# Token rows split into fp16 halves before storing, and turned by DMA transposes instead of TensorE, in the two mixture layers of a gated cross-attention kernel

## What is computed

```python
x = x + tanh(g_xattn[0]) * L0_xattn(layernorm(x), ctx)    # linear attention
x = x + tanh(g_ffn[0])   * L0_ffn(layernorm(x))           # 8 experts, top 2
x = x + tanh(g_xattn[1]) * L1_xattn(layernorm(x), ctx)    # softmax attention, int8 rounding
x = x + tanh(g_ffn[1])   * L1_ffn(layernorm(x))           # 16 experts, top 4
# a mixture layer, x: [2048, 256]
logits = x @ router_w.T
weights, ids = top_k(softmax(logits))
routed = sum_e w[:, e] * ((silu(x @ gate[e]) * (x @ up[e])) @ down[e])     # inner width 176
shared = sigmoid(x @ shared_gate) * ((silu(x @ sgate) * (x @ sup)) @ sdown) # inner width 704
out = routed + shared
```

## Time and profile before

| | |
|---|---|
| median of three runs | 952.78 us |
| the profiled execution: its own time | 959.28 us |
| its span, first to last instruction | 957.5 us |
| PE matmul busy | 746.1 us (78%), 5700 instructions |
| DVE busy | 686.8 us (72%) |
| ACT busy | 443.4 us (46%) |
| POOL busy | 505.3 us (53%) |
| granted TensorE clock, mean | 0.843 of full |
| DMA, mean | 127 GB/s, 121.17 MB in all |

### The profile page before, as it was taken

The page is one execution under the profiler, slowest core; times in us unless marked ns, Lnnn a source line. Parts: engine busy times, 40 slices in busy tenths (PEclk is TensorE's granted clock), DMA queues, the critical chain, the costliest instruction groups (busy, mean ns, idle before and its releaser), DMA issues.

```text
span 957.5 us, 18420 instructions
## 1 busy us (share of the span) xinstructions
PE 746.1 (78%) x5700; PEld 496.1 (52%) x5701; DVE 686.8 (72%) x1825; ACT 443.4 (46%) x1037; POOL 505.3 (53%) x607
## 2 busy tenths in 40 slices
PE   3469749678988797677777777659879999977994
PEld 1258635456664454344444444335657777754563
DVE  4868947756775777988887888738857777734467
ACT  3355335123332233888887878725123444422331
POOL 6284974566636557553554347010054545478883
PEclk9679876789999899697767676657979999978998
DMA  8034444624542213898889988821034444446444
GB/s 287 1 92 157 157 157 147 187 80 142 164 127 89 66 34 81 146 191 160 151 163 168 182 159 162 148 75 40 0 93 137 136 136 140 142 123 143 79 79 141
DMA packets 205754, 121.17 MB, mean 127 GB/s; under 512 B 146476, under 2 KB 197808, under 8 KB 205680
## 3 DMA queue, kind: packets, MB, share of 16 engines
q1 hardware_dynamic: 192816, 91.10, 39.2%
q0 software_dynamic: 12864, 29.14, 12.5%
HBM read 64.16 MB, written 32.98 MB: 101 GB/s over the span
## 4 chain that ended last, share of the span: by engine, by line
PE 35%; DVE 11%; ACT 7%; issue 6%; DVEq 4%; DMA 3%; another core or an unknown queue 2%; POOL 1%; POOLq 0%; ACTq 0%
PE PS L269 18%; PE PS L852 4%; DVE sb_wk L1450 4%; PE PS L791 3%; ACT sb_xnf L1417 3%; DMA sb_xnf<-sb_xnf 3%; PE PS L1344 2%; ACT sb_wkh L1417 2%; PE PS L815 2%; PE PS L844 2%; PE PS L407 1%; DVEq L250 1%; DVE sb_x_sb L942 1%; DVE sb_x_sb L948 1%
## 5 line engine op out<-in xcount | busy, mean ns | idle before, releaser
L673 POOL DMA_INDIRECT sb_xnf<-token_table,sb_ids x120 | 115.8, 965 | 148.7 <-DVE sb_wk L1018 62.8
L1450 DVE TENSOR_SCALAR_CACHE_REDUCE sb_wk<-PS 128x512 f16<-128x512 f32 x256 | 161.9, 684 | 3.8 <-PE PS L1344 3.8
L269 PE MATMUL PS<-sb_xnT,sb_sgu 128*128 128x512 f16 x528 | 129.5, 398 | 1.1 <-DVE sb_lg L455 0.6
L269 PE MATMUL PS<-sb_region,sb_wkh 128*128 x720 | 122.6, 321 | 4.8 <-issue 3.1
L1417 ACT ACTIVATE sb_xnf<-PS,sb_slotv 128x512 int16<-128x512 f32 x128 | 86.8, 689 | 25.5 <-DVE sb_wk L1450 21.4
L875 ACT ACTIVATE sb_wk<-PS 128x512 f32<-128x512 f32 (+1 forms) x48 | 28.6, 596 | 144.6 <-PE PS L269 123.7
L269 PEld LDWEIGHTS PS<-sb_region,sb_wkh 128*128 128x128 f16 x720 | 69.7, 100 | 47.0 <-issue 13.9
L1417 ACT ACTIVATE sb_wkh<-PS,sb_slotv 128x512 int16<-128x512 f32 x128 | 86.6, 690 | 12.4 <-DVE sb_wk L1450 9.6
L852 PE MATMUL PS<-sb_region,sb_wkh 128*128 x600 | 78.3, 277 | 8.9 <-DVE sb_wa L1031 7.3
L269 PEld LDWEIGHTS PS<-sb_xnT,sb_sgu 128*128 128x128 f16 x528 | 53.0, 102 | 60.7 <-issue 10.9
L791 PE MATMUL PS<-sb_sdn,sb_wkh 128*128 128x256 f16 x544 | 70.8, 282 | 17.4 <-DVE sb_wkh L989 15.2
(11 more groups left out here) (296 smaller groups left out, 1717.3 us busy)
## 6 DMA issues: line engine op xcount, KB each, us to landing
slot_table<-sb_wa SPq DMA_DIRECT2D x60, 256.0 KB
slot_table<-token_table SPq DMA_DIRECT2D x16, 640.0 KB
sb_stg<-gu SPq DMA_DIRECT2D x24, 352.0 KB
sb_stg<-dn SPq DMA_DIRECT2D x24, 256.0 KB
token_table<-sb_xnf SPq DMA_DIRECT2D x16, 256.0 KB, 4.7
sb_stg<-sgu SPq DMA_DIRECT2D x8, 352.0 KB
sb_x_sb<-x SPq DMA_DIRECT2D x1, 2048.0 KB, 12.3
out<-sb_x_sb SPq DMA_DIRECT2D x16, 128.0 KB
```

Of the source, the lines that this page charges most:

```text
L269: last = nc.tensor.matmul(out_, lhs(i, c), rhs(j, c), start=(c == 0 and n == 0 and not begun), stop=(c == C - 1 and n == 2 and not more))
L673: nc.gpsimd.indirect_dma_start(xg[l][:, 2 * (g % XR) + n, :], None, xw[l][:, :], bass.IndirectOffsetOnAxis(ap=ids[:, 2 * g + n:2 * g + n + ...
L1450: nc.vector.tensor_scalar(h_any[(2 * s + h) % 6], PS[:, (2 * s + h) % LB, :], LEVELS, None, ALU.add, ALU.min, accum_out=h_nb[s % 3][:, h:h ...
```

## The change

The rows are split into a high and a low fp16 half as rows, before they are stored: ACT and DVE normalise into a buffer `wk1`, ACT copies the high halves into `xnf` (now seen as fp16, 256 high and 256 low columns per token), DVE subtracts. SP then turns each pair of tiles (128 x 1024 fp16) with one DMA transpose into `xnT`, in the place of PE's transposes and of the two passes out of PSUM; after all eight it stores the rows. In the experts' loop the gathered row holds both halves, so SP turns the two tiles of a group with two DMA transposes (128 x 512 fp16 each) into a ring of four buffers, and PE's transposes, ACT's line 894 and DVE's line 1002 go. The turned product and the result get two PSUM banks each.

```diff
         def route_pe(pe, l):
             n = E[l] + 1
-            for j in range(NT // 2 + 1):
-                if j < NT // 2:
-                    at_least(pe, r_xn[l], 0, j + 1)
-                    at_least(pe, r_xd[l], 0, j + 1)
-                    at_least(pe, r_xl[l], 0, j - 1)
-                    for c in range(C):
-                        for i in range(2):
-                            last = nc.tensor.transpose(PS[:, j % 2, c * TB + i * P:c * TB + (i + 1) * P],
-                                                       xnf[:, 2 * j + i, c * P:(c + 1) * P], idf[:, :])
-                    last.then_inc(r_xT[l].sem, 1)
...
+            for j in range(NT // 2):
+                at_least(pe, x_turned[j % 4][l], 0, 16 * (j // 4 + 1))
+                at_least(pe, r_lgc[l], 0, j - 3)
+                for i in range(2):
+                    t = 2 * j + i
+                    last = mm3(PS[:, j % 4, i * n:(i + 1) * n], lambda h, c: x_cols[:, t, h, c, :],
+                               lambda h, c: rw[l][:, h, c, :])
+                last.then_inc(r_lg[l].sem, 1)
         def route_act(act, l):
...
                     t = 2 * j
-                    nc.scalar.activation(xnf[:, t, :], x_sb[:, t, :], ACT.Identity, bias=nmr[:, t:t + 1],
+                    at_least(act, r_xl[l], 0, j - 3)
+                    nc.scalar.activation(wk1[:, j % 4, 0:D], x_sb[:, t, :], ACT.Identity, bias=nmr[:, t:t + 1],
                                          scale=rstd[:, t:t + 1]).then_inc(r_xn[l].sem, 1)
                 if j >= 1:
-                    at_least(act, r_xT[l], 0, j)
-                    nc.scalar.activation(xnT[:, 0, :, (j - 1) * TB:j * TB],
-                                         PS[:, (j - 1) % 2, :].rearrange("p (c n) -> p c n", c=C), ACT.Copy).then_inc(r_xh[l].sem, 1)
+                    at_least(act, r_xn[l], 0, j)
+                    at_least(act, r_xd[l], 0, j)
+                    nc.scalar.activation(x_rows[:, 2 * j - 2:2 * j, 0, :], wk1[:, (j - 1) % 4, :].rearrange("p (t n) -> p t n", t=2),
+                                         ACT.Copy).then_inc(r_xh[l].sem, 1)
         def route_dve(dve, l):
...
                     at_least(dve, r_xh[l], 0, j + 1)
-                    nc.vector.tensor_tensor(xnT[:, 1, :, j * TB:(j + 1) * TB], PS[:, j % 2, :].rearrange("p (c n) -> p c n", c=C),
-                                            xnT[:, 0, :, j * TB:(j + 1) * TB], ALU.subtract).then_inc(r_xl[l].sem, 1)
+                    nc.vector.tensor_tensor(x_rows[:, 2 * j:2 * j + 2, 1, :], wk1[:, j % 4, :].rearrange("p (t n) -> p t n", t=2),
+                                            x_rows[:, 2 * j:2 * j + 2, 0, :], ALU.subtract).then_inc(r_xl[l].sem, 1)
         def table_dma(sp, l):
             for j in range(NT // 2):
-                at_least(sp, r_xn[l], 0, j + 1)
-                at_least(sp, r_xd[l], 0, j + 1)
+                at_least(sp, r_xh[l], 0, j + 1)
+                at_least(sp, r_xl[l], 0, j + 1)
+                at_least(sp, x_turned[j % 4][l], 0, 16 * (j // 4))
+                sp.dma_start_transpose(x_turns[:, 2 * j:2 * j + 2].rearrange("p t g n -> p (t g) n"),
+                                       x_rows[:, 2 * j:2 * j + 2].rearrange("p t h n -> p (t h n)")).then_inc(x_turned[j % 4][l].sem, 16)
+            for j in range(NT // 2):
                 sp.dma_start(token_rows(xw[l], 2 * j, 2, slice(0, D)), xnf[:, 2 * j:2 * j + 2, :]).then_inc(stored[l].sem, 16)
         def rows_dma(sp, l):
+            def turn(g):
+                at_least(sp, e_ld[l][g % XR], 0, 32 * (g // XR + 1))
+                at_least(sp, e_gu[l], 0, g + 1 - XR)
+                if g == 0:
+                    at_least(sp, s_d[l], 0, HALF)
+                for n in range(2):
+                    sp.dma_start_transpose(xT[g % XR][:, 2 * C * n:2 * C * (n + 1), :],
+                                           xg[l][:, 2 * (g % XR) + n, 0:D].bitcast(F16)).then_inc(e_xT[l][g % XR].sem, 16)
+            for g in range(XR):
+                turn(g)
+            if l == 1:
+                sp.wait_ge(table_zeroed, 16 * ZERO_PARTS)
             for g in range(NG[l]):
+                if g + XR < NG[l]:
+                    turn(g + XR)
                 at_least(sp, e_y[l], 0, g + 1)
@@ ffn_pe
-                               lambda j, c: xnT[:, j, c, b * 512:(b + 1) * 512])
+                               lambda j, c: x_cols[:, 4 * b:4 * b + 4, j, c, :])
...
-                if inside(base, s, 0, NG[l] - 1):
-                    transposes(base, s + 1)
                 if inside(base, s, 0, NG[l]):
                     e = experts(base, s)
-                    at_least(pe, e_xl[l], base, s + 1)
+                    at_least(pe, e_xT[l][s % XR], base * 8, 32 * (s // XR + 1))
                     for n in range(2):
-                        last = mm3(PS[:, 2 * u + n, 0:EG], lambda i, c: wkh[:, 2 * u + i, (2 * n + c) * P:(2 * n + c + 1) * P],
+                        last = mm3(PS[:, 2 * u + n, 0:EG], lambda i, c: xT[s % XR][:, 2 * C * n + C * i + c, :],
                                    lambda h, c: GU[l][:, bass.ds(e[n], 1), h, c, :].rearrange("p o n -> p (o n)"))
@@ block.sync
             table_dma(sp, 1)
-            sp.wait_ge(table_zeroed, 16 * ZERO_PARTS)
             rows_dma(sp, 1)
```

More of the change, by code:

```diff
@@ L289, in gated_flamingo @@
         r_xn = both("r_xn", NT // 2)
-        r_xT = both("r_xT", NT // 2)
+        x_turned = [both(f"x_turned{u}", 32) for u in range(4)]
         r_xh = both("r_xh", NT // 2)
@@ L333, in gated_flamingo @@
         e_ld = list(zip(*(both(f"e_ld{u}", 32 * len(range(u, NG[0], XR))) for u in range(XR))))
+        e_xT = list(zip(*(both(f"e_xT{u}", 32 * len(range(u, NG[0], XR))) for u in range(XR))))
         e_st = list(zip(*(both(f"e_st{u}", 16 * len(range(u, NG[0], 2))) for u in range(2))))
@@ L351, in gated_flamingo @@
         yr = [xnf_flat[:, r * 2 * D:(r + 1) * 2 * D].rearrange("p (k d) -> p k d", d=D) for r in range(CR)]
-        y_sum = [w[:, n * D:(n + 1) * D] for w, tiles in ((stg_flat, 8), (wqp32, 4), (xnf_flat[:, 12 * D:16 * D], 4))
+        y_sum = [w[:, n * D:(n + 1) * D] for w, tiles in ((stg_flat, 8), (wqp32, 4), (wkv32, 4))
                  for n in range(tiles)]
@@ L809, in ffn_pe @@
             at_least(pe, r_ids[l], 0, 1)
-            def transposes(base, s):
-                at_least(pe, e_ld[l][s % XR], base * 8, 32 * (s // XR + 1))
-                for n in range(2):
-                    for c in range(C):
-                        last = nc.tensor.transpose(PS[:, 4 + s % 2, (2 * n + c) * P:(2 * n + c + 1) * P],
-                                                   xg[l][:, 2 * (s % XR) + n, c * P:(c + 1) * P], idf[:, :])
-                last.then_inc(e_xT[l].sem, 1)
             def experts(base, s):
@@ L843, in group @@
                         for c in range(C):
-                            last = nc.tensor.transpose(PS[:, 6, (2 * c + n) * P:(2 * c + n + 1) * P],
+                            last = nc.tensor.transpose(PS[:, 5 - u, (2 * c + n) * P:(2 * c + n + 1) * P],
                                                        wk1[:, 3 - u, n * EI + c * P:n * EI + (c + 1) * P], idf[:, :])
@@ L856, in group @@
                     last.then_inc(e_d[l].sem, 1)
-            transposes(0, 0)
             steps(pe, NG[l] + 2, XR, XR, 3, group)
@@ L1093, in gated_flamingo @@
         q_iT = [w.bitcast(F16).rearrange("p (g n) -> p g n", n=P) for w in
-                (*(xnf[:, 12 + 2 * u:14 + 2 * u, :].rearrange("p t d -> p (t d)") for u in range(2)), xn32[:, 10 * D:12 * D])]
+                (*(xnf[:, 12 + 2 * u:14 + 2 * u, :].rearrange("p t d -> p (t d)") for u in range(2)), xn32[:, 14 * D:16 * D])]
         h_h = [wkh[:, 2 * u:2 * u + 2].rearrange("p a b -> p (a b)") for u in range(4)] + \
```

81 lines of the change are left out of this document (36 added, 45 removed).

## The result

The changed kernel takes 993.62 us in the median (990.41 to 1000.21, 4 runs), the kernel before 952.29 beside it: ratio 1.0434 (95% interval 1.0373 to 1.0494). It is slower, as forecast, but by 41 us where 10 were forecast, outside the range of 951 to 977. The profiled execution took 992.78 us, its span is 991.0.

The account below looks back on a forecast made before the run. PE was taken to bound layer 1's loop, POOL layer 0's, SP's queue order layer 0's routing. +22.5 - 0.5 + 1 + 0.7 - 13.7 = +10.0 us, put on the median 952.78: 963 us, range 951 to 977.

Parts of the forecast that it names:

- Routing of layer 0: Layer 0's transposes wait behind fills and loads in SP's order; logits at 182.7 instead of 154.7, 28 us late.
- Row numbers +22.5: Layer 0's row numbers come at 214.2, not 191.65: +22.5 us, between +18 and +26.
- Loop of layer 0: Layer 0's experts' loop: POOL is the bound and keeps 4.3 us a group; only -0.5 us, for the last group.
- The second rival: Layer 0's routing: fills don't hold SP, transposes go out early, kernel faster, about 943 if at 160; chance 0.06.
- Routing of layer 1: Layer 1's routing: SP is free, logits at 652.7 to 654.9 against 652.15; +1 us taken, 0 to +3.
- the two prices: Cost of one 128 x 1024 transpose: 1.23 us on SP's queue, 1.54 us with the DMA engines full.
- Loop of layer 1: Layer 1's experts' loop: PE is the bound; period 3.96 to 3.58 us, -13.7 us, with 0.7 more at its start.
- The part on DMA: Layer 1's loop: DMA needs 3.40 us a group, 97% busy at 3.52; period 3.58 taken, share above 0.8.
- The loop of layer 1 gains nothing: Rival: gather, transpose and head of line on SP make a chain of four periods of 3.96; +24, 977; chance 0.12.
- A half-size transpose costs as much as a full one: Rival, both experts' loops: 1.54 us for each half-size transpose, 4.94 us a group; about +76, 1029; chance 0.04.
- The tail: Stage 846 to 878, where PE is busy 20.1 of 32 us: taken as it is, no change.

Follow-up runs that it names:

- Both experiments on the queue: Changed kernel, layer 0's transposes issued earlier in SP's queue: 982.41 us; with stores and first four weight loads also ahead of the last zero fills: 972.41 us.
- its queue is mended: Changed kernel with layer 0's eight transposes, table stores and first four weight loads issued by SP ahead of the last four zero fills: 972.41 us, ratio 1.0168.
- a version 0.7% faster: Kernel before, PE's loop unrolled by eight steps, six of eight down products reusing gate and up's loaded registers: 953.36 us, ratio 0.9933.

## Why the prediction was right and wrong

**Routing of layer 0: right.** "The first can't be issued before 165.8": 165.80. Last transpose 182, logits 182.7: the last logits are copied at 183.27. Row numbers +22.5: the first gather is +19.8, since the steps from logits to row numbers took 28.0 us (183.27 to 211.32) where 31.5 were put. Both experiments on the queue confirm the reason, not only the number. The second rival (SP early) is what the kernel becomes if its queue is mended, and even then it isn't faster (1.0168).

**Loop of layer 0: wrong by 6.9 us.** "POOL keeps its 4.3 us" took POOL's 2.2 to 2.6 us at the drain for POOL's own. They depend on something outside POOL: with the transposes, all or half of them, they grew to 3.3 to 4.0, in every third group. From first gather to last gate and up the loop lost 6.4 us where 0.5 was to be gained. "No other engine releases it" had been read as "it is constant".

**Routing of layer 1: too cheap.** Its start is 23.4 us later than before. Less that, the first transpose goes out at 640.55 (forecast 640.1) and the last logits are copied at 655.3, where 652.7 to 654.9 were the bounds: +3.3, not +1, and outside 0 to 3. The timeline of SP's queue:
```profile
663.95 11.28 SPq L638 DMA_TRANSPOSE sb_xnT<-sb_xnf  x8
```
That is 1.41 us each, between the two prices. The stages between the two loops, combining and attention, were 2.8 us shorter than before, so that the step from layer 0's last gate and up to layer 1's first gather came out nearly as forecast (+1.2 where +1 stood), by luck.

**Loop of layer 1: the step that failed.** It is "PE: 3.96 - 0.44 = 3.52 us, or 3.41 if the gap goes as well", and from it "0.38 x 36 groups = -13.7 us". Measured: 4.23 to 4.26, and from the first gather to the first combining one the lateness grows from 27.4 to 39.8: +12.4, where -13.0 stood. That is a miss of 25.4 us; with layer 0's 6.9, the 2.7 of its routing the other way, 0.2 between, and the tail's 6.3 the other way, it makes the 23.5 us between forecast and spans. The subtraction took all the time between PE's waits for matmuls. PE's sequence also has two register loads a group, and what the change took from PE was what stood over one of them. With that load left out the period is 3.64. A sign stood in the prediction's own reading: its parts, 1.96, 0.44, 1.10, 0.44 and 0.11, add up to 4.05 and not to 3.96, since 1.96 holds time that the next record shares.

Uncovering the load doesn't explain all of it. Four transposes can cover no more than their 0.44 us, and without cover the period would have stayed at 3.87. It rose to 4.23. From the start of the last matmul ahead of gate and up to that of gate and up, the changed kernel needs 0.88 us in the mean of the window, the kernel before 0.21: 0.23 more than the transposes can account for; most of the rest stands ahead of the down product (0.20 instead of 0.11). The further 0.36 us of the period goes when the load goes, but why the load costs more in the changed kernel isn't shown. With half of the transposes the 0.88 is 0.76, so their traffic may have a part; the register arithmetic of the new wait behind the load wasn't tested by itself.

The part on DMA was sound: a period of 3.58 and a share above 0.8 were forecast for it, and 3.64 and 0.94 were measured, with turned rows arriving just in time.

**The rivals.** "The loop of layer 1 gains nothing" came nearer than the forecast, 3.96 and 977 where 4.23 and 994 were measured, with the wrong chain: gather, transpose and SP's head of line weren't what PE waited for. "A half-size transpose costs as much as a full one" is true of SP's queue, 1.24 us, which had the room, and false of the engines, about 0.7. SP getting to the transposes early is what mending the queue makes of the kernel, and even so it is 1.7% slower than before.

The two prices of the Trainium skill: VectorE: DVE Perf Modes, section "The three transpose paths", gives 1309 ns for 128 x 128 by DMA, by which the eight blocks of a group would need 10.5 us; the trace disagrees: with the load left out, a group with its eight blocks took 3.64 us in all. Advanced Engine Details and Errata, section "X-Bar Transpose (TRN2)", gives 350 to 400 GB/s; the trace disagrees too: 128 KB in about 0.7 us of all engines are some 190 GB/s.

**The tail** gave back 6.3 us between the first combining gather and the end. PE's idle time of 846 to 878 is gone (28.2 of 32 us busy in the last of the windows above), and the prediction had left it as it was. It isn't the change that gave it back. The kernel before has the stalls without an event in that stretch, up to 7.3 us each, and its version without the load has none; there the same way from first combining gather to end takes 105.6 us, in the changed kernel 105.8, in the kernel before 112.1. Over all runs it is 104.3 to 105.8 us without such stalls and 111.7 to 113.5 with them. So the 6.3 us belong to what this one execution of the kernel before met, and this may also be why it was 7.0 us above its median and why the two medians lie further apart than the two spans; what the stalls are stays open.

## What to carry to other kernels

Before taking work off a busy engine, ask what that engine's queue does beside its matmuls: register loads take time of its sequence too, and cheap matmuls may be what hides them. Test it by leaving a load out in the kernel you have; here that is what led to a version 0.7% faster. And a transfer put into a queue has two prices, its place behind what stands there (20 us at the first gather here, all but 1.3 of it gone with another order) and what the rest of the program pays beside it: 4.8 us in layer 0's loop.

## What the runs showed of the hardware that I had not expected

- A load of two numbers into PE's registers costs at least 0.59 us a group in the changed kernel (4.23 to 3.64), 0.12 in the kernel before (3.87 to 3.75), and moving it only moves the gap.
- An engine shown as 89.3 of 90 us busy ran 3% faster without such a load.
- POOL's wait ahead of the third part of a split rose from 2.2 to 2.6 us to 3.3 to 4.0 with SP's transposes under way, as much with half of them (3.6 to 3.9), and fell back to 2.2 to 2.7 without them.
- The queue time of a DMA transpose on SP is the same for 128 KB and 256 KB, 1.24 and 1.23 us, while the engines' time goes from 1.54 us to about 0.7.
